# Long convolutions in Toeplitz blocks of 64 on four 64x64 tiles of TensorE instead of blocks of 128 on the whole array

## The reference

```python
xn = layernorm(x)
proj = xn @ in_proj_w + in_proj_b            # 3 * 256 columns
v = proj[..., :256]
for i in range(2):                           # two orders
    h = implicit_filter(...)                 # [2048, 256], decays as exp(-|decay| * lag)
    v = fft_conv(v, h)                       # causal, one filter a channel
    v = v * gated_control(proj[..., (i+1)*256:(i+2)*256])   # 3 taps, 256x256 gate, sigmoid
attn = v @ out_proj_w + out_proj_b
r = relu(bitlinear(xn, w_fc) + gate * (xn @ v.T @ fast_b.T @ u.T))   # 1024 hidden
out = x + attn + bitlinear(r * r, w_proj)
```

## Time and profile before

| | us |
|---|---|
| three runs | 1172.95, 1154.29, 1172.76 |
| median | 1172.76 |
| profiled execution | 1176.48 |
| its span (first to last instruction) | 1174.8 |
| mean granted TensorE clock | 0.949 of 2.4 GHz |

### The profile page before, as it was taken

How to read it: one execution, slowest core, us unless ns; L and a number is a source line. 1 busy time by engine, 2 the same in 40 slices (tenths; PEclk the granted TensorE clock), 3 DMA queues, 4 the chain that set the end, 5 groups by cost and what they waited for, 6 DMA issues and landing times. The chain is left out here.

```text
span 1174.8 us, 21456 instructions
## 1 busy us (share of the span) xinstructions
PE 1056.6 (90%) x6948; PEld 942.7 (80%) x6949; DVE 624.5 (53%) x1031; ACT 434.6 (37%) x598; POOL 235.2 (20%) x267
## 2 busy tenths in 40 slices
PE   6768999999973999999999999999999999997597
PEld 3357788877863989889898898898898999997586
DVE  7848999999982333333343342342343443343486
ACT  5326777777771222222221122122222222221573
POOL 1044556545601001101101101100101101100011
PEclk9869999999996999989998899998999999999799
DMA  6253323332316888887886897977977877888297
GB/s 168 114 197 127 127 94 138 143 125 92 124 72 218 191 221 191 201 224 147 207 206 158 207 217 192 237 183 164 232 204 176 226 192 189 215 189 266 80 373 266
DMA packets 123605, 214.09 MB, mean 182 GB/s; under 512 B 14212, under 2 KB 101268, under 8 KB 122292
## 3 DMA queue, kind: packets, MB, share of 16 engines
q1 hardware_dynamic: 111572, 168.46, 56.0%
q0 software_dynamic: 11568, 42.08, 9.8%
q10 hardware_dynamic: 432, 3.15, 0.7%
HBM read 164.11 MB, written 49.54 MB: 182 GB/s over the span
## 5 line engine op out<-in xcount | busy, mean ns | idle before, releaser
L999 PEld LDWEIGHTS py<-V,T 128*128 128x128 f32 x3072 | 375.9, 195 | 48.8 <-issue 38.3
L999 PE MATMUL py<-V,T 128*128 x3072 | 373.5, 275 | 30.7 <-DMA T<-filters 30.3
L923 DVE TENSOR_TENSOR r<-r 128x512 f32<-128x512 f32 x128 | 88.6, 692 | 345.3 <-ACT r L951 345.3
L951 ACT ACTIVATE r<-pf 128x512 f32<-128x512 f32 x128 | 76.5, 597 | 461.5 <-PE pf L400 450.4
L925 DVE TENSOR_TENSOR r_lo<-r,r_hi 128x512 fp32r<-128x512 f32 x128 | 92.6, 724 | 89.2 <-ACT r_hi L954 89.2
L984 PE MATMUL pp<-wproj,r_hi 128*128 128x256 f32 x512 | 139.1, 305 | 0.0
L984 PE MATMUL pp<-wproj,r_lo 128*128 128x256 f32 x512 | 129.6, 286 | 0.0
L954 ACT ACTIVATE r_hi<-r 128x512 fp32r<-128x512 f32 x128 | 80.8, 631 | 97.1 <-DVE r L923 97.1
L398 PE MATMUL pf<-xm_hi,wfc_hi 128*128 x256 | 111.9, 437 | 0.7 <-DMA xm_hi<-xnT_hbm 0.5
L582 DVE SCALAR_TENSOR_TENSOR xc<-ctrl,taps,xc 128x512 f32<-128x512 f32 x128 | 99.8, 799 | 17.3 <-ACT xc L653 16.1
L439 POOL TENSOR_SCALAR xt<-xt,norms 128x256 f32<-128x256 f32 x64 | 107.2, 1687 | 3.4 <-POOL norms L433 3.4
(11 more groups left out here) (163 smaller groups left out, 1646.6 us busy)
## 6 DMA issues: line engine op xcount, KB each, us to landing
T<-filters SPq DMA_DIRECT2D x256, 384.0 KB, 6.3
xt<-in_attn_x SPq DMA_DIRECT2D x16, 512.0 KB, 4.1
xnT_hbm<-xn_hi SPq DMA_DIRECT2D x16, 512.0 KB, 4.3
xnT_hbm<-xn_lo SPq DMA_DIRECT2D x16, 512.0 KB, 3.8
gc_hbm<-xc SPq DMA_DIRECT2D x16, 512.0 KB, 2.6
xm_hi<-xnT_hbm POOLq DMA_DIRECT2D x16, 512.0 KB, 5.4
xm_lo<-xnT_hbm POOLq DMA_DIRECT2D x16, 512.0 KB, 8.1
xb<-in_attn_x POOLq DMA_DIRECT2D x16, 512.0 KB, 9.6
```

The lines of the kernel that those rows point to most:

```text
L923: dve.tensor_tensor(r[j][:, :], r[j][:, :], r[j][:, :], ALU.mult).then_inc(sq_done, 1)
L951: act.activation(r[j][:, :], pf[j][:, :], ACT.Relu).then_inc(relu_done, 1)
L999: last = pe.matmul(y[:, c, :, A:NA], tile[:, j * P:(j + 1) * P], V[:, bass.ds(m * (GPI * GC) + (g * GC + c), 1), :, 0:NA - A] .rearrange(" ...
```

## The change

It keeps the mathematics and the interleaving of the mix stage, and puts the convolution on 64x64 tiles of the array.

- `V` and `GC1` become [128, 128, batch, 32 blocks of 64]: the partitions 0 to 63 hold one half of the channels, 64 to 127 the other.
- A group is still eight channels: two row halves (`side`) x two column halves (`q`) x two (`PAIR`). Always done are five blocks of 64 (`NEAR`), where flagged two more (`MID`) for all eight channels. Each block is a float32 matmul of 64 rows, 64 columns and 4 * (32 - A) moving columns: 128, 124, 120, 116, 112. Matmuls that follow one another alternate the row half; the two row halves write different PSUM banks.
- `T` is double-buffered by group: two DMAs a group load 5 blocks of its eight channels, a group ahead, and `Tmid` with them.
- ACT copies the moving operands to `vwin` a group ahead.
- PE's order in a group: the first half of the convolution (l = 0), middle blocks, `fc(2g)`, `proj(2g-1)`, `fc(2g+1)`, the second half (l = 1), `proj(2g)`.
- In the project stage the values are computed by plain float32 matmuls of 128 rows, 64 columns and 128 moving columns, 32 a chunk, from a new copy `xnT` that ACT makes before the high part; the low part is made from `xnT`. `xc` is stored in blocks of 64 with its two halves mixed.
- The row of scales goes over HBM; flags are one bit a group; loads of the second gate and the output weights become two DMAs each.

```diff
-NEAR = 3
-MID_FROM = (NEAR - 1) * P + 1
-FAR_FROM = NEAR * P + 1
+BW = 64
+SIDES = P // BW
+SLOTS_V = D // SIDES
+TB = CH // BW
+NB = L // BW
+NEAR = 5
+MID = 2
+MID_FROM = (NEAR - 1) * BW + 1
+FAR_FROM = (NEAR + MID - 1) * BW + 1
...
@@ project stage, ACT @@
                     if s0 >= 0:
+                        act.wait_ge(v_mm, s + 1)
+                        act.wait_ge(xn_split, s + 1)
+                    act.activation(xnT[:, :, :], pT[:, :, :], ACT.Copy).then_inc(xnT_done, 1)
+                    if s0 >= 0:
                         act.wait_ge(xn_saved[0], 16 * s + 16)
                     act.activation(xn[0][:, :, :], pT[:, :, :], ACT.Copy).then_inc(xn_hi_done, 1)
@@ project stage, PE @@
-                    for i in range(TT):
-                        ts = slice(i * P, (i + 1) * P)
+                    pe.wait_ge(xnT_done, s + 1)
+                    for i in range(TB):
+                        ts = slice(i * BW, (i + 1) * BW)
                         for k in range(KT):
-                            last = split_mm(pe, pn[:, i, :], (xn[0][:, k, ts], xn[1][:, k, ts]),
-                                            (Win[0][:, k, 0:D], Win[1][:, k, 0:D]), k == 0, k == KT - 1)
+                            for side in range(SIDES):
+                                last = pe.matmul(pn[side * BW:(side + 1) * BW, i, :].rearrange("p (h c) -> p h c", h=KT),
+                                                 xnT[:, k, ts], Wv_sides[:, k, :, side, :], start=(k == 0), stop=(k == KT - 1))
...
@@ mix stage @@
-        T = sb("T", [P, TILES, TC, NEAR * P])
-        Tmid = sb("Tmid", [P, GC, P])
+        T = [sb(f"T{i}", [P, SIDES * PAIR, NEAR * BW]) for i in range(2)]
+        Tmid = [sb(f"Tmid{i}", [P, SIDES * PAIR, MID * BW]) for i in range(2)]
+        vwin = [sb(f"vwin{i}", [P, SIDES, PAIR, B, NB]) for i in range(2)]
-        py = [ctx.enter_context(nc.psum_tensor(f"py{i}", [P, GC, B, NA], F32)) for i in range(2)]
+        py = [ctx.enter_context(nc.psum_tensor(f"py{i}", [P, SIDES, 2 * PAIR, B, NB], F32)) for i in range(2)]
...
@@ mix stage, SP @@
+                        wait_alone(sp, group_mm, G + 1, sp_passed)
+                        load(T[g % 2], 0, NEAR, T_loaded[g % 2])
+                        middle = sp.value_load(flag[0:1, bass.ds(G + 1, 1)], min_val=0, max_val=1)
                         with sp.If(middle > 0):
+                            load(Tmid[g % 2], NEAR, MID, mid_loaded[g % 2])
...
@@ mix stage, ACT @@
+            def window(order, m, it, g):
+                G = it * GPI + g
+                act.wait_ge(group_mm, G + 1)
+                if order:
+                    act.wait_ge(y_out, G - GROUPS // ORDERS + 3)
+                act.activation(vwin[g % 2][:, :, :, :, :].rearrange("p b l n a -> p b l (n a)"),
+                               Vs[:, :, bass.ds(channels(m, g), PAIR), :], ACT.Copy).then_inc(window_done, 1)
...
@@ mix stage, PE @@
                             for A in range(A0, A0 + count):
                                 j = A - A0 if order else A0 + count - 1 - A
-                                last = pe.matmul(y[:, c, :, A:NA], tile[:, j * P:(j + 1) * P],
-                                                 V[:, bass.ds(m * (GPI * GC) + (g * GC + c), 1), :, 0:NA - A]
-                                                 .rearrange("p c n a -> p (c n) a"),
-                                                 start=(c == 0 and A == 0), stop=True, skip_group_check=True)
+                                for q in range(SIDES):
+                                    for side in range(SIDES):
+                                        rows = slice(side * BW, (side + 1) * BW)
+                                        last = pe.matmul(py[g % 2][q * BW:(q + 1) * BW, side, l, :, A:NB],
+                                                         tile[rows, q * PAIR + l, j * BW:(j + 1) * BW],
+                                                         vwin[g % 2][rows, q, l, :, 0:NB - A],
+                                                         start=(l == 0 and A == 0), stop=True, skip_group_check=True)
                             return last
...
+                        conv(T[g % 2], 0, 0, NEAR)
...
                         fc(it, 2 * g, m % 2)
-                        near(1)
                         if g > 0:
                             proj(it, 2 * g - 1)
                         fc(it, 2 * g + 1, m % 2)
-                        near(2)
-                        near(3)
+                        conv(T[g % 2], 1, 0, NEAR).then_inc(group_mm, 1)
                         proj(it, 2 * g)
```

More of the change, by code:

```diff
@@ L171, in _ @@
             load(proj_t, projT.rearrange("p (m d) -> p m d", m=HT), stored)
-            sp.wait_ge(stored, 16 * 9)
+            sp.wait_ge(srow_ready, 1)
+            load(scales, srow[0:1, :], stored)
+            sp.wait_ge(stored, 16 * 12)
             sp.wait_ge(proj_in, 16 * PROJ_LOADS)
@@ L817, in lags, with channels @@
         def lags(order, A0, count):
-            return P * (NA - A0 - count) if order == 0 else P * A0
+            return BW * (NB - A0 - count) if order == 0 else BW * A0
+        def channels(m, g):
+            return m * (GPI * PAIR) + g * PAIR
         @block.sync
         def _(sp):
-            sp.sem_inc(tile_mm, TILES)
-            sp.sem_inc(mid_loaded, 16)
+            sp.sem_inc(group_mm, 2)
+            for i in range(2):
+                sp.sem_inc(mid_loaded[i], 16 * SIDES)
             tail = sp.value_load(flag[0:1, 0:1], min_val=0, max_val=1)
@@ L840, in body, with load @@
-                        middle = sp.value_load(flag[0:1, bass.ds(G + 1, 1)], min_val=0, max_val=2 ** TILES - 1)
+                        def load(buf, A0, count, s):
+                            first = lags(order, A0, count)
+                            for side in range(SIDES):
+                                row = channels(m, g) * SIDES + (order * D + side * SLOTS_V)
+                                sp.dma_start(buf[side * BW:(side + 1) * BW], hankel[:, bass.ds(row, SIDES * PAIR), first:first + count * BW]).then_inc(s, 16)
@@ L854, in loads @@
+                            sp.sem_inc(mid_loaded[g % 2], 16 * SIDES)
+                        if far:
+                            wait_alone(sp, group_mm, G + 2, sp_passed)
+                            for j in range(FARS):
+                                load(T[1 - g % 2], NEAR + MID + NEAR * j, NEAR, far_loaded)
+                                wait_alone(sp, far_used, G * FARS + (j + 1), sp_passed)
                 groups(sp, order, body)
@@ L1014, in body @@
                         with pe.If(middle > 0):
-                            pe.wait_ge(mid_loaded, G * 16 + 32)
-                            for q in range(TILES):
-                                with pe.If(middle // 2 ** q % 2 > 0):
-                                    for c in range(q * TC, q * TC + TC):
-                                        conv(Tmid[:, c, :], c, NEAR, 1)
-                        for j in range(FAR if far else 0):
-                            pe.wait_ge(far_loaded, G * (16 * FAR) + 16 * (j + 1))
-                            for c in range(TC):
-                                last = conv(T[:, 1, c, :], (j % TILES) * TC + c, NEAR + 1 + NEAR * (j // TILES), NEAR)
+                            wait_alone(pe, mid_loaded[g % 2], it * (GPI * 8 * SIDES) + (g // 2 + 2) * (16 * SIDES), pe_passed)
@@ L1024, in body @@
+                            for l in range(PAIR):
+                                conv(Tmid[g % 2], l, NEAR, MID)
+                        for j in range(FARS if far else 0):
+                            wait_alone(pe, far_loaded, G * (16 * SIDES * FARS) + 16 * SIDES * (j + 1), pe_passed)
+                            for l in range(PAIR):
+                                last = conv(T[1 - g % 2], l, NEAR + MID + NEAR * j, NEAR)
                             last.then_inc(far_used, 1)
                         fc(it, 2 * g, m % 2)
-                        near(1)
```

243 lines of the change are left out of this document (129 added, 114 removed).

## The result

| | before | after |
|---|---|---|
| median, us | 1171.01 (1154.29 to 1172.95, 4 runs) | 1035.58 (1031.01 to 1038.81, 4 runs) |
| profiled execution, us | 1176.48 | 1038.81 |
| its span, us | 1174.8 | 1037.2 |
| mean granted clock, of 2.4 GHz | 0.949 | 0.961 |
| PE, PEld busy, us | 1056.6, 942.7 | 893.6, 727.1 |

The ratio is 0.891 [0.880, 0.903]: 11% faster, where 3.5% was forecast. The nearest case was the one with a chance of 0.07, all four tiles at once, at 1004.

A forecast was written before the change was run, and what follows sets the result against it. PE was taken to set the pace in mix and project, its convolution records bound by weight loads. Terms -67 + 34 - 30 + 13 + 10 - 1 = -41 gave 1135.5 profiled, about 1132 us median (-3.5%); range 1055 to 1295.

The forecast's parts named there:

- all four tiles at once: Rival, convolution: 27 ns a record, 2.16 us a group, -195 us, total 1004 us; chance 0.07.
- The convolution: Mix stage: 80 records a group at 52 ns, overlapping in pairs, 4.16 us against 5.20; -67 us.
- The weight load: Convolution: records before bound by loads of 128 weight columns, 108 ns; a block of 64 should load in 54 ns.
- Switches: Mix stage: four a group between whole array and tiles, 0.13 us each; +34 us (0 to 69), upper end 0.27 us each.
- Waits and clock: Mix stage: most waits for `T` and middle blocks, and the low clock behind them, go; -30 us (-15 to -43).
- what is late next is `proj`: Mix stage: relu to low part takes 2.7 us, last `proj` of a chunk has 3.1 us between; priced at nothing.
- Middle blocks: Mix stage, flagged groups: all eight channels done, 32 records, 1.7 us, 11 times, less 5; +13 us.
- Project and the start of mix: Project stage: longer value projection, switches and an ACT copy, +10 us (+2 to +20); first `T` of mix larger, +1.
- column halves don't overlap: Rival, project stage: value projection goes one by one, 6.86 us instead of 3.46, +54 us, total 1186; chance 0.19.
- Loads that wait in a row half: Rival, convolution: a load waits for the matmul, 77 ns a record, +61 instead of -67, total 1287; chance 0.13.
- no overlap: Rival, convolution and value projection: nothing overlaps, 101 ns a record, 8.08 us a group, +184, total 1436; chance 0.11.
- a low clock in tiled stretches: Rival, mix stage: tiled stretches get 1.2 GHz; low in a third +194, total 1326, in all 1700; chance 0.07.

The follow-up runs named there:

- a2: Changed kernel with only the order of a half's matmuls altered: all five lags of one tile in a row, then the next tile; 1236.94 us (one run).
- b1: Changed kernel with half of `proj(2g-1)` put into the second half of the convolution, 96 switches more, same work; 1031.05 us (one run).
- c1: Changed kernel with the flag's check for middle blocks moved from before `fc(2g)` to behind it; median 1006.02 us.
- c3: Changed kernel with both convolution halves in one stretch after `fc(2g)`, `proj(2g-1)`, the check and `fc(2g+1)`, then `proj(2g)`; median 956.64 us.
- a4: Changed kernel with only matmul order altered: one row half after the other, column halves alternating through all five lags; 1086.7 us (one run).
- v1: Changed kernel with the value projection doing all 16 matmuls of one column half, then all of the other, instead of alternating; 1082.04 us (one run).

## Why the prediction was wrong

**The convolution** (forecast -67, measured -193). This step failed, in the sentence "The two passes of a matmul are on the same tile and follow one another, and the next matmul is on the other row half. If matmuls start in order and a tile has one at a time, the second pass of one can run beside the first pass of the next, never more: 50 ns a record". The second pass does follow the first on its tile; but it waits there, in one of three places, and the matmuls behind it pass it by and start on the other tiles (a2, with 692 ahead of 786). Four tiles, each some 100 ns a record: 25.9 ns, where the forecast had 52. The reason given against the rival with 1004 us, "two passes on one tile in a row", was the same sentence, and it is why that rival had 0.07. The forecast had a warning in the earlier trace rows, where weight loads already run beside the matmul ahead of them, and didn't carry it over to matmuls.

The Trainium skill, TensorE: Matmul & The Clock Gate, section The mechanism, says that matmuls are strictly first in, first out, with no reordering. The trace of a2 differs, and the measurement decides. TensorEngine Tiling (Array Packing), section Tiling Modes, of the Trainium skill says that different tiles load weights and multiply in parallel; the runs agree, in bursts of four 7 ns apart and in 40 loads a microsecond.

**The weight load.** That loads of 128 columns bound the kernel before (108 ns) fits its trace: the second record of a piece starts 55 ns after the first, what 64 columns take by the forecast's 0.837 ns, and the later ones are 108 to 118 ns apart whatever their columns, as are the starts of the loads (106 to 112). No run isolates it, since none has a narrow load with as few moving columns. After, loads bound nothing: 40 in 1.00 us, 25 ns each, where the forecast worked out 54 for one of 64 columns; in the trace four start within 20 ns and each lasts about 130, so loads of different tiles run side by side too.

**Switches** (+34 forecast, +23 measured). 0.09 us each by all four transitions and by b1, inside the range of 0 to 0.27. The upper end, an emptied pipeline, does not show: a `proj` record lasts 280 ns (its end is modelled), and the first tiled record starts 209 after it. It is a third of 0.27. By the Trainium skill, TensorEngine Tiling (Array Packing), section Tiling Modes, a change of tiling mode drains the engine; these starts don't show it. The 0.10 in the 0.27 was also misread: the piece of 1.54 us in the earlier trace rows has no idle time ahead of it, it follows a `proj` record that starts 0.18 us before. A half also begins with one distance of 160 ns for 109, which is counted with the convolution.

**Waits and clock** (-30 forecast, +28 measured). The waits that were named went as forecast in part: `T` 3.5 us less by the distances, those ahead of middle blocks 5, and the low clock fell from 44.5 to 11.1 us. New ones took their place, +23 for the flag's check ahead of `fc` and +18 at and inside `proj` for `r_lo`. The prediction named the second ("what is late next is `proj`") with 0.4 us to spare; that reserve was counted with halves of 2.1 us, and they lasted 1.0. The check it didn't name at all. Both come of the same error: an engine that is faster than forecast uncovers what lay beside it. a2 shows that: with halves of 3.06 us, and all else the same, every step to `fc` and to `proj` takes 184 or 185 ns, the seams without any wait, and the profile has no wait of PE in that stage. In the kernel before, too, a step to `fc` behind a check took 90 ns. The distances inside `fc`, which has less low clock, are the rest. c1 and c3 show the size: 31 us by moving the check, 80 with one stretch besides.

**Middle blocks** (+13). Their records went from 5.2 to 8.5 us, +3, by the same 23 ns; the forecast's 1.7 us a group took 52 ns a record. **Fewer pieces** of convolution (two for three a group) were not counted and gave about 9 us.

**Project and the start of mix** (+10 and +1). The last transposes are 5 us later (329.6 for 324.4), and the wait for the first `T` is 3.7 longer (22.27 for 18.59): mix starts 9.6 later, and output is 0.8 longer. Project thus took about half of its +10; the start of mix took more than the 1 it had. The value projection lasts 3.44 us from its first start to its last, forecast 3.46. `vwin` cost nothing, as forecast.

**The rivals.** That column halves don't overlap fell with a4 and the value projection; its price was sound (+54 worked out, +46 in the one run of v1, which made it so). Loads that wait in a row half, no overlap, and a low clock in tiled stretches fell with the 25.9 ns and the clock of 0.98.

**Sum.** -193 + 23 + 28 + 3 - 9 + 10 = -138; the spans differ by 137.6. In the rival's own sum (1004) only the convolution was right; it too had counted the waits as gone.

## What to carry to other kernels

Order 64x64 matmuls so that no tile gets more than four records in a row (a float32 matmul is two); whether rows or columns alternate made no difference here. Before pricing a faster piece, list what runs beside it (a flag read and a branch of 1.0 us, an elementwise chain of 2.7) and price that without the cover. Where a piece becomes short, join its parts: one stretch instead of two saved switches and waits, 49 us here beyond the 31 of the moved check.

## What was unexpected of the hardware

- Starts on TensorE are not in program order across tiles. Records are handed out 7 ns apart; a tile runs one and three wait at it: this rule reproduces the five lengths of a half within 0.03 us (1.00, 1.69, 3.06, and, worked out before the runs, 1.06 and 1.81).
- Pairs of tiles that share their rows are as fast as pairs that share their columns: 1.69 us each.
- A switch between the whole array and 64x64 tiles adds 0.09 us to the distance of two records (209 for 118 ns into the tiles), a third of the forecast's estimate for an emptied pipeline.
- A flag's value read by PE takes 302 ns, and with the branch behind it 1.0 us of its stream.
